# One term of a softmax denominator: slot 16 of three head groups summed by VectorE into the key sum instead of by TensorE with a column of ones

## The chip, the cores and the metric

One core of one Trainium2 chip. The metric is the device time of one execution in microseconds; less is better. Engines are called TensorE (PE in the rows; PEld is its weight load), VectorE (DVE), ScalarE (ACT), GpSimd (POOL) and SyncE (SP, here only a queue for transfers).

## What is computed

A post-norm transformer block on 2048 tokens of width 512 in float32. The part that matters here is the attention:

```python
qkv = (x @ w_qkv).reshape(B, S, 3, H, D)          # S = 2048, H = 16 heads, D = 32
q, k = _unit_norm(q), _unit_norm(k)               # and rotary embedding on the even heads
logits = jnp.einsum('bshd,bthd->bhst', q, k) * q_gain[None, :, None, None]
logits = jnp.where(causal[None, None], logits, jnp.finfo(logits.dtype).min)
attn = jax.nn.softmax(logits, axis=-1)
y = jnp.einsum('bhst,bthd->bshd', attn, v).reshape(B, S, Dm)
x = _layernorm(x + y @ w_out)
```

After it comes a mixture of experts (8 routed, top 2, and one shared) and a second layer norm. The change doesn't touch them.

## The kernel before

The 16 heads are worked on in four **groups** of four heads (g = 0 to 3). In a group, the 2048 queries are taken in four **steps** of 512 (i = 0 to 3), and the keys in blocks of 128 (j). A pair of a step and a key block is a **slot**. Causality leaves 4, 8, 12 and 16 key blocks for the four steps, so a group has 40 slots; `STEP_AT` gives the first slot of each step (0, 4, 12, 24) and `ORDER` the order of key blocks in a step. Slots 12 to 23 are the third step. Slot 16 is key block 4 of it, with all 512 queries and no mask.

For each slot:

- TensorE makes the **scores** of four heads, transposed: keys on partitions, 512 queries along the free axis (`pe_scores`, lines 1503 to 1534; the matmuls are line 1529). They go to two halves of PSUM, two heads each; the half p of a slot waits for the exponential of the same half of the slot before.
- ScalarE takes the **exponential** of each half into one of four buffers of `probs` (`act_exp`, lines 1669 to 1684). Before it overwrites a buffer it waits for the value matmuls and, by `sum_dve`, for the VectorE add of the slot four before.
- TensorE multiplies with v (`pe_values`, lines 1561 to 1582; line 1579), one slot behind the scores: its order is scores of slot n, projections and turns of this slot, values of slot n - 1.

The softmax also needs the **sum over the keys**, which lie on partitions and in many slots. A slot contributes in one of three ways:

- *Direct* (in `DIRECT`, or `DIRECT_LAST` for the last group): four matmuls with a block of ones (line 1576), ahead of the value matmuls, add its column sums into `sums_ps` in PSUM. A float32 matmul shows as two instructions, so there are eight.
- The first slot of a step that isn't direct is *first*: ScalarE writes its exponentials straight into `key_sum` instead of `probs`.
- Every later one that isn't direct is *added*: VectorE does `key_sum += probs` over four heads (`dve_add_keys`, lines 1800 to 1809; 128x2048 elements for a full slot).

At the end of a step TensorE adds `key_sum` into `sums_ps` with ones (`pe_sums`, line 1588), after waiting for the last VectorE add of the step, and ahead of the values of the last slot. In the third step slot 12 is direct, slot 13 is first, slots 14, 15 and 17 to 22 are added, and 16 and 23 are direct. The last group has another list, where 16 is added already.

Each engine runs a program of its own, slot by slot, written out in fixed tables:

- VectorE (lines 1860 to 1877): in a slot first the low half of a turned tile (`dve_turn_low`, line 1797; in groups 1 and 2 at slots 16 and 23, in group 0 at 16 and 24), then at the start of a step the reading and inverting of the sums (lines 1811 to 1829), the rotation, the add of the slot, the norms, and at slot 23 the high half of the split of the **next group's projection weights** (`dve_split_w`, line 1728).
- GpSimd: at slot 23 the causal mask on that slot's exponentials (`pool_mask`, line 1558), then the low half of the weight split (`pool_split_w`, line 1886), which waits for VectorE's high half. Masks of slots 20, 21 and 22 are made by TensorE (`MASK_BY_PRODUCT`, line 1532).
- TensorE: at slot 25 the first projection of the next group (`pe_project`, lines 1466 to 1484): three parts of four matmuls, the third of which waits for the low half of the weights.
- SyncE's queue: at slot 18 the load of those weights, and zero fills of a scratch tensor at slots 20 to 23.

The constants count too: `added(g, slot)` (line 1352) gives the value of `sum_dve` that each engine waits for, from the same lists.

Of the kernel before, what the change touches and what calls it, by code (L numbers as in the profile page):

```python
# [80 lines left out]

DIRECT = {0, 1, 2, 3, 4, 12, 16, 23, 24, 33, 37, 38, 39}
DIRECT_LAST = {0, 1, 2, 3, 5, 12, 13, 22, 24, 31, 32, 33, 38}
ADDING = [i for i in range(NC) if any(n not in DIRECT for n in range(STEP_AT[i], STEP_AT[i + 1]))]

# [14 lines left out]
def direct_of(g):  # L100

    return DIRECT_LAST if isinstance(g, int) and g == NG - 1 else DIRECT

# [50 lines left out]
def build(nc, x, x_across, w_qkv, w_out, q_gain, gate_w, w_gate, w_up, w_down, sw_gate, sw_up, sw_down,  # L154
          rope_cos, rope_sin, numbers, out):
    with ExitStack() as ctx:
# [1195 lines left out]
        def added(g, slot):  # L1352

            return (SLOTS - len(DIRECT) - len(ADDING)) * g + sum(n not in direct_of(g) and not is_first(g, n) for n in range(slot + 1))

        def is_first(g, slot):

            return slot not in direct_of(g) and slot == first_added(g, step_of(slot)[0])
# [598 lines left out]
```

How the kernel before makes its waits and increments, by code:

```python
        def load_piece(sp, lot, piece):  # L460
            if lot == 1:
                sp.wait_ge(lot0_low, piece + 1)
            if 1 < lot < LOTS - 1:
                sp.wait_ge(ffn_low, PIECES * (lot - 2) + piece + 1)
            if lot == LOTS - 1:
                sp.wait_ge(ffn_low, PIECES * (lot - 2) + (2, 3, 5)[piece])
            src, start = weights_of(lot)[piece], raw_at(lot, piece)
            to, n = raw[:, start:], src.shape[1]
            if piece < 2:
                sp.dma_start(to[:, 0:KC * n].rearrange("p (k n) -> p k n", k=KC), src.rearrange("(k p) n -> p k n", p=P)).then_inc(ffn_loaded[piece], 16)
            else:
                sp.dma_start(to[:, 0:2 * D].rearrange("p (k n) -> p k n", k=2), src[0:2 * P].rearrange("(k p) n -> p k n", p=P)).then_inc(ffn_loaded[piece], 16)
                for p0 in (0, MIXED) if lot == 0 else (0,):
                    sp.dma_start(to[p0:p0 + src.shape[0] - 2 * P, 2 * D:3 * D], src[2 * P:]).then_inc(ffn_loaded[piece], 16)
# [1 line left out]
        def tail_sync(sp):  # L477
            for n in range(2):
                sp.wait_ge(y_stored[n], 16 * NC * NG // 2)
            sp.wait_ge(y_ready, NC * NG)
            for t in range(TPC, 2 * TPC):
                load_x_row(sp, t)
            for t in range(2 * TPC, NT):
                if t >= TPC + 8:
                    sp.wait_ge(x1_ready, t - 7)
                load_x_row(sp, t)
                if t == 2 * TPC:
                    sp.wait_ge(sums_done, len(ADDING) * NG)
```

## Time and profile before

| | us |
|---|---|
| median of 3 runs | 1038.64 (1038.08 to 1041.03) |
| the profiled execution's own time | 1034.4 |
| its span, first to last instruction | 1032.7 |
| TensorE busy in the span | 999.6 (97%) |
| VectorE busy | 651.0 (63%) |
| ScalarE busy | 547.3 (53%) |
| GpSimd busy | 376.6 (36%) |

The profile is of one execution. "Busy" counts the time in which an engine has an instruction in work; matmuls are pipelined, so a busy TensorE is not one at its peak. "Idle before" is the time that an engine stood still ahead of an instruction, and the name behind it is what ended that. The chain of waits follows the work back from its last instruction to what released each step.

### The profile page before, as it was taken

How to read it: one execution, taken by the hardware profiler on the slowest of the kernel's cores; microseconds unless marked ns; L12 is line 12 of the kernel's file. 1: busy time of each engine (PE TensorE's matmuls, PEld its weight loads, DVE VectorE, ACT ScalarE, POOL GpSimd, SP SyncE). 2: the span in 40 equal slices, each digit the busy share in tenths (PEclk: the TensorE clock that was granted, in tenths of full speed). 3: DMA queues.
4: the chain of work that ended last, by engine and by line, in shares of the span. 5: the costliest groups of instructions: out<-in, count | busy, mean ns of one | idle time of the engine just before them, and what ended most of it. 6: DMA issues, size and time to landing. Idle time of an engine off the chain costs nothing.

```text
span 1032.7 us, 17543 instructions
## 1 busy us (share of the span) xinstructions
PE 999.6 (97%) x5951; PEld 724.4 (70%) x5951; DVE 651.0 (63%) x1138; ACT 547.3 (53%) x906; POOL 376.6 (36%) x312
## 2 busy tenths in 40 slices
PE   6899999999999999999999999999999999999996
PEld 7564566646666455664367778889999999998885
DVE  5699584896849968398679666444334333324776
ACT  4778776687767867668846632223333333321213
POOL 0332132321323312131534107563475666424431
PEclk9999999999999999999999999999999999999998
DMA  6447333473342723418146206593455553414433
GB/s 205 129 117 213 95 103 97 108 215 92 102 132 84 224 73 102 123 52 252 44 129 188 78 31 229 191 289 120 156 166 166 166 168 116 145 53 126 135 110 123
DMA packets 115821, 140.60 MB, mean 136 GB/s; under 512 B 10272, under 2 KB 74016, under 8 KB 115744
## 3 DMA queue, kind: packets, MB, share of 16 engines
q1 hardware_dynamic: 83552, 102.56, 33.4%
q10 hardware_dynamic: 27072, 20.20, 6.2%
q0 software_dynamic: 5120, 16.78, 5.0%
q8 instruction: 52, 0.85, 0.4%
q14 instruction: 25, 0.20, 0.1%
HBM read 83.93 MB, written 55.57 MB: 135 GB/s over the span
## 4 chain that ended last, share of the span: by engine, by line
PE 77%; DVE 10%; ACT 6%; DMA 2%; POOL 2%; issue 2%; SPq 0%; DVEq 0%; ACTq 0%
PE scores L634 15%; PE scores L1529 10%; PE bank L1482 10%; PE scores L694 8%; PE bank L1579 8%; PE bank L622 8%; PE bank L739 5%; PE scores L542 4%; ACT probs L1683 4%; DVE key_sum L1808 4%; PE bank L1576 3%; DVE x L1164 1%; PE scores L602 1%; POOL wqkv_l L1886 1%; PE bank L1588 1%
## 5 line engine op out<-in xcount | busy, mean ns | idle before, releaser
L1683 ACT ACTIVATE probs<-scores,shift_now 128x1024 f32<-128x1024 f32 (+3 forms) x296 | 273.5, 978 | 74.1 <-PE scores L1529 48.8
L1808 DVE TENSOR_TENSOR key_sum<-key_sum,probs 128x2048 f32<-128x2048 f32 (+1 forms) x96 | 205.3, 2138 | 50.7 <-PE bank L1579 19.1
L1529 PEld LDWEIGHTS scores<-q_stack,k_stack 96*128 96x128 f32 x624 | 99.2, 188 | 121.6 <-ACT probs L1683 66.1
L1529 PE MATMUL scores<-q_stack,k_stack 96*128 96x512 f32 (+3 forms) x624 | 177.1, 396 | 6.6 <-ACT probs L1683 2.8
L1579 PE MATMUL bank<-probs,v_sb 128*32 128x512 f32 (+3 forms) x1184 | 135.8, 533 | 0.0
L634 PE MATMUL scores<-ffn_w,xt_h 128*128 (+1 forms) x608 | 125.1, 328 | 0.0
L1044 DVE TENSOR_TENSOR ht_l<-scores,ht_h 128x256 fp32r<-128x256 f32 x39 | 16.6, 425 | 142.2 <-ACT ht_h L827 142.2
L634 PEld LDWEIGHTS scores<-ffn_w,xt_h 128*128 128x128 f32 x608 | 101.0, 189 | 3.5
L1263 POOL TENSOR_TENSOR ffn_w<-raw,ones 128x1408 fp32r<-128x1408 f32 (+4 forms) x32 | 64.1, 2014 | 97.6 <-PE bank L622 78.7
L1558 POOL TENSOR_SCALAR_AFFINE_SELECT probs<-probs 128x512 f32<-128x512 f32 x40 | 44.3, 1115 | 136.4 <-ACT probs L1683 136.4
L694 PE MATMUL scores<-x1T_h,ffn_w 128*128 128x512 f32 x352 | 89.5, 391 | 0.0
L1267 POOL TENSOR_TENSOR ffn_w<-raw,ffn_w 128x1408 fp32r<-128x1408 f32 (+3 forms) x31 | 80.3, 2600 | 1.9
L694 PEld LDWEIGHTS scores<-x1T_h,ffn_w 128*128 128x128 f32 x352 | 65.7, 188 | 13.5
L881 ACT CAST hid_h<-silu 128x512 fp32r<-128x512 f32 (+1 forms) x24 | 14.9, 620 | 105.7 <-DVE silu L1080 105.7
L622 PE MATMUL bank<-ffn_w,ht_h 128*128 (+2 forms) x234 | 67.6, 397 | 0.7 <-issue 0.7
L1579 PEld LDWEIGHTS bank<-probs,v_sb 128*32 128x32 f32 x1184 | 29.7, 109 | 47.0 <-issue 39.3
L634 PE MATMUL scores<-ffn_w,xt_l 128*128 (+1 forms) x304 | 61.0, 322 | 0.0
L834 ACT COPY y_tile<-bank 128x512 f32<-128x512 f32 x39 | 22.9, 587 | 69.3 <-PE bank L622 58.9
L1786 POOL TENSOR_TENSOR rope_prod<-qk_even,sin 128x128 f32<-128x128 f32 x8 | 4.5, 557 | 142.9 <-DVE qk_even L1775 142.9
L739 PE MATMUL bank<-ffn_w,hid_h 128*128 128x512 f32 x176 | 54.8, 394 | 1.4 <-DVE x L1132 1.1
L1327 POOL DMA_INDIRECT extra<-y_sorted,place_int x32 | 32.3, 1008 | 55.8 <-DMA y_sorted<-y_tile 20.9
L1482 PE MATMUL bank<-wqkv_h,xT_h 128*128 128x384 f32 x232 | 51.4, 343 | 0.9 <-DVE xT_l L1723 0.7
(254 smaller groups left out, 1760.2 us busy)
## 6 DMA issues: line engine op xcount, KB each, us to landing
k_stack<-turn_scratch SPq DMA_DIRECT2D x48, 256.0 KB, 4.3
q_stack<-turn_scratch SPq DMA_DIRECT2D x45, 256.0 KB, 3.9
x_sorted<-zeros SPq DMA_DIRECT2D x39, 256.0 KB, 3.5
y_sorted<-y_tile ACTq DMA_DIRECT2D x39, 256.0 KB, 2.9
x_tile<-x_sorted ACTq DMA_DIRECT2D x148, 64.0 KB, 2.0
turn_scratch<-turned_h SPq DMA_DIRECT2D x31, 256.0 KB, 2.1
turn_scratch<-turned_l SPq DMA_DIRECT2D x31, 256.0 KB, 2.3
raw<-w_gate SPq DMA_DIRECT2D x8, 704.0 KB, 5.2
```

Of the source, the lines that this page charges most:

```text
L622: mm = nc.tensor.matmul(out_tile[:], hs[0:kn, k, :], moving(slots[j - 1], DOWN + (low * 3 + k) * D, D, kn), start=(m == 0 and k == 0), sto ...
L634: mm = nc.tensor.matmul(to[:, 0:FH], xs[:, k, :], moving(slot, first + (low * KC + k) * FH, FH), start=(m == 0 and k == 0), stop=(m == 2 a ...
L694: mm = nc.tensor.matmul(scores[:, which, n % 2, :], stationary(half, slot, which, low, k, hc), xs[:, k, c * CH:(c + 1) * CH], start=(m == ...
L739: mm = nc.tensor.matmul(bank[n % 2][:], hs[:, k, tt * P:(tt + 1) * P], shared_down(half, slot, low, k), start=(k == 0 and hs is hid_h and ...
L1263: last = nc.gpsimd.tensor_tensor(high, src, one, ALU.mult)
L1267: last = nc.gpsimd.tensor_tensor(low, src, high.bitcast(F32), ALU.subtract)
L1482: mm = nc.tensor.matmul(qkv_bank(n)[:, 0:3 * P], xs[:, k, tok], ws[:, k, :], start=(m == 0 and k == 0), stop=(m == 2 and k == KC - 1))
L1529: mm = nc.tensor.matmul(scores[:, p, hh, lo:CH], k_stack[0:3 * HD, h, j * P:(j + 1) * P], q_stack[0:3 * HD, i % 2, h, lo:CH], start=True, ...
L1558: nc.gpsimd.affine_select(out=block, in_=block, compare_op=ALU.is_ge, fill=0.0, base=0, pattern=[[0, HG], [1, P]], channel_multiplier=-1). ...
L1579: mm = nc.tensor.matmul(y_ps[HD * h:HD * (h + 1), lo:CH], v_sb[:, j, HD * h:HD * (h + 1)], exponents(g, slot)[:, h, lo:CH], start=(slot == ...
L1683: nc.scalar.activation(exponents(g, slot)[:, 2 * p:2 * p + 2, lo:CH], scores[:, p, :, lo:CH], ACT.Exp, bias=shift_now[:, p:p + 1]).then_in ...
L1808: nc.vector.tensor_tensor(key_sum[:, :, lo:CH], key_sum[:, :, lo:CH], probs[:, slot % 4, :, lo:CH], ALU.add).then_inc(sum_dve, 1)
```

## The change

Slot 16 leaves the list of direct slots of the first three groups. By that alone its ones matmuls (line 1576) go from TensorE's program, and an add (line 1808) comes into VectorE's, between those of slots 15 and 17 and behind the turned tile of slot 16.

```diff
-DIRECT = {0, 1, 2, 3, 4, 12, 16, 23, 24, 33, 37, 38, 39}
+DIRECT = {0, 1, 2, 3, 4, 12, 23, 24, 33, 37, 38, 39}
 DIRECT_LAST = {0, 1, 2, 3, 5, 12, 13, 22, 24, 31, 32, 33, 38}
```

## Rows read from the trace of the kernel before

**Rows 1.** The page: busy time by engine, and the chain that ended last.

```profile
PE 999.6 (97%) x5951; PEld 724.4 (70%) x5951; DVE 651.0 (63%) x1138; ACT 547.3 (53%) x906; POOL 376.6 (36%) x312
...
PE 77%; DVE 10%; ACT 6%; DMA 2%; POOL 2%; issue 2%; SPq 0%; DVEq 0%; ACTq 0%
```

**Rows 2.** Windows, slots 12 to 23 of group 2: length, busy PE, PEld, DVE, ACT, POOL; clock, DMA.

```profile
327.00:357.00 30.00, 29.67 (x202) 12.49 (x202) 27.85 (x37) 25.40 (x31) 5.67 (x7) 1.00 0.60 173
```

**Rows 3.** Timeline, slots 14 to 22 of group 2: start, us, engine, line, operation.

```profile
337.98 5.01 DVE L1808 TENSOR_TENSOR key_sum<-key_sum,probs 128x2048 f32<-128x2048 f32 x2
...
341.75 1.06 PE L1576 MATMUL bank<-probs,ones 128*32 128x512 f32 x8
...
342.63 1.04 PE L1579 MATMUL bank<-probs,v_sb 128*32 128x512 f32 x8
...
343.60 1.21 PE L1529 MATMUL scores<-q_stack,k_stack 96*128 96x512 f32 x4
343.62 2.29 DVE L1808 TENSOR_TENSOR key_sum<-key_sum,probs 128x2048 f32<-128x2048 f32 x1
344.46 3.24 ACT L1683 ACTIVATE probs<-scores,shift_now 128x1024 f32<-128x1024 f32 x3 [0.87 <-PE scores L1529]
...
346.61 10.39 DVE L1808 TENSOR_TENSOR key_sum<-key_sum,probs 128x2048 f32<-128x2048 f32 x5 [0.69 <-ACT probs L1683]
```

**Rows 4.** The chain of waits, group 2, slots 19 to 25: start, us, what.

```profile
349.04 2.30 DVE key_sum L1808
...
357.61 0.88 DVE wqkv_h L1728
...
358.56 3.49 POOL wqkv_l L1886
```

**Rows 5.** Timeline, group 2, slots 23 to 27.

```profile
357.71 1.06 PE L1588 MATMUL bank<-key_sum,ones 128*32 128x512 f32 x8
...
362.09 0.97 PE L1482 MATMUL bank<-wqkv_l,xT_h 128*128 128x384 f32 x4 [0.33 <-POOL wqkv_l L1886]
...
369.28 2.29 DVE L1808 TENSOR_TENSOR key_sum<-key_sum,probs 128x2048 f32<-128x2048 f32 x1 [6.69 <-PE bank L1579]
```

**Rows 6.** Timelines of VectorE and TensorE, group 0, slots 18 to 25.

```profile
93.04 10.39 DVE L1808 TENSOR_TENSOR key_sum<-key_sum,probs 128x2048 f32<-128x2048 f32 x5 [0.68 <-ACT probs L1683]
103.35 1.39 DVE L1728 CAST wqkv_h<-wqkv_raw 128x1536 fp32r<-128x1536 f32 x1
...
108.38 0.96 PE L1482 MATMUL bank<-wqkv_l,xT_h 128*128 128x384 f32 x4 [0.24 <-POOL wqkv_l L1886]
```

**Rows 7.** Timeline of VectorE, group 1, slots 18 to 22.

```profile
220.13 2.29 DVE L1808 TENSOR_TENSOR key_sum<-key_sum,probs 128x2048 f32<-128x2048 f32 x1 [0.48 <-ACT probs L1683]
222.91 7.97 DVE L1808 TENSOR_TENSOR key_sum<-key_sum,probs 128x2048 f32<-128x2048 f32 x4 [0.48 <-DVE key_sum L1808]
```

**Rows 8.** GpSimd's mask, group 0; VectorE's cast by line; adds by form; adds in group 2.

```profile
102.78 1.15 POOL L1558 TENSOR_SCALAR_AFFINE_SELECT probs<-probs 128x512 f32<-128x512 f32 x1 [15.40 <-ACT probs L1683]
...
L1728 DVE CAST wqkv_h<-wqkv_raw x4: 950/956/1389, 6.7 to 357.5; 128x1536 fp32r<-128x1536 f32 x4
...
L1808 DVE TENSOR_TENSOR key_sum<-key_sum,probs 128x1536 f32<-128x1536 f32 x8 | 14.1, 1758 | 1.5 <-POOL probs L1558 0.5
...
319.18 7.01 DVE L1808 TENSOR_TENSOR key_sum<-key_sum,probs 128x2048 f32<-128x2048 f32 x3
```

**Rows 9.** TensorE's waits and its clock: timeline, then windows (columns as in rows 2).

```profile
428.22 1.19 PE L1529 MATMUL scores<-q_stack,k_stack 96*128 96x512 f32 x4 [2.16 <-DMA q_stack<-turn_scratch]
...
430.00:432.00 2.00, 2.00 (x21) 0.78 (x16) 0.00 (x0) 1.19 (x2) 0.00 (x0) 0.50 0.57 161
...
430.00:440.00 10.00, 10.00 (x71) 5.26 (x62) 5.10 (x13) 6.73 (x10) 0.00 (x0) 0.86 0.40 107
...
183.62 0.50 PE L1529 MATMUL scores<-q_stack,k_stack 96*128 96x256 f32 x2 [1.45 <-DMA k_stack<-turn_scratch]
...
183.00:189.00 6.00, 5.38 (x35) 4.15 (x36) 5.83 (x11) 3.48 (x5) 4.04 (x6) 1.00 0.23 66
```

## The prediction

> **What bounds the kernel now.** I read the page first. TensorE is busy for 97% of the span, and the chain that ended last is 77% TensorE but also 10% VectorE [rows 1]. So TensorE time is worth something on average, and the question is whether it is worth anything where slot 16 stands. The stretches come next: in the 30 us of slots 12 to 23 of the third head group TensorE is busy 29.67 us and VectorE 27.85 us at full clock [rows 2]. Two engines are close to full at the same time, so no share can decide; only the waits can.
>
> The timeline around slot 16 of the third group shows both sides [rows 3]. TensorE runs the ones matmuls of slot 16 from 341.75, the value matmuls from 342.63 and the scores of slot 18 from 343.60; ScalarE idles 0.87 us before the exponential of slot 18. That idle time is the ones matmuls' doing. VectorE finishes its two adds of slots 14 and 15 at 342.99 (337.98 + 5.01), does the low half of a turned tile, starts the add of slot 17 at 343.62, idles only 0.69 us and then runs five adds (slots 18 to 22) without a break for 10.39 us.
>
> The chain of waits says which side counts after that [rows 4]. After slot 18's exponential it is no longer on TensorE: it follows the key_sum adds to the last one, then the split of the next group's weights on VectorE, then the 3.49 us GpSimd half of that split. Then TensorE, which had waited for that weight [rows 5], carries on. The other two groups have the same row of adds, with other slack in front of it [rows 6, 7]. VectorE is therefore the bound from slot 18 to slot 25 in exactly the three groups that change.
>
> **The change, part by part.**
>
> Removed: in each of three groups the ones matmuls of slot 16, eight instructions that take 0.88 us of TensorE's order (341.75 to 342.63) [rows 3]; they overlap, so their spacing is the price and not the duration of one. Up to slot 23 TensorE and ScalarE gain it: the exponential of slot 18 loses its 0.87 us wait. Slot 12 stays the first direct slot of its step and slot 13 the first one in key_sum, so no start flag and no owner of key_sum moves. No DMA is added, removed or moved in any queue. The last group has a list of its own, in which 16 was already absent, and doesn't change.
>
> Added: one 128x2048 add in each of three groups. The add of slot 17 takes 2.29 [rows 3]. Of the five that run back to back the first starts at 346.61 and the second at 349.04 [rows 3, 4], 2.43 later, so a gap of some 0.13 belongs to each. The new add costs 2.42 in all. Its operand is long ready (the ones matmuls of slot 16, which read the same exponentials, started at 341.75), so it stands right before the add of slot 17, with no wait of its own.
>
> Behind it on VectorE are queued the adds of slots 17 to 22, the turned tile, the weight split, and the reading of the sums. What absorbs the 2.42 is the idle time before those adds, less the usual 0.13 each. Third group: 0.69 - 0.13 = 0.56 before slot 18, none later; the last add ends 1.86 later. First group: 0.68 - 0.13 = 0.55 [rows 6], 1.87 later. Second group: 0.48 - 0.13 = 0.35 before slot 18, and the same again before slot 19 [rows 7]. That second idle follows an add directly and nothing explains it; if it vanishes in a full queue the shift is 1.72, if it stays 2.07. I take 1.72.
>
> Buffers: the exponential of slot n needs the add of slot n - 4. With ScalarE 0.87 earlier and VectorE 1.86 later, slot 24 would start at about 356.6 and needs the add of slot 20, which ends at about 355.6. The margin is 1 us, so that wait costs nothing; if ScalarE didn't gain, it would be larger still.
>
> First consumer, **the sum over key_sum** (line 1588). In the third group it starts at 357.71 [rows 5]. TensorE would now arrive at 356.8, but the add of slot 22 ends at 357.00 + 1.86 = 358.86 (357.00 is 346.61 + 10.39). So it starts about 1.2 later than before, and TensorE idles 2 us: the 0.88 gained is gone here.
>
> Second consumer, **the weight split**. VectorE's cast and then GpSimd's subtraction follow the last add in order, so GpSimd ends at 358.56 + 3.49 + 1.86 = 363.9 [rows 4]. TensorE's third part of the projection started at 362.09, after waiting [rows 5]; without the wait of 0.33 and with the late sum it would be due at 361.8 + 1.2 = 363.0, so it waits for GpSimd again, 0.9 us, and starts 1.86 late. Everything behind it (values of slot 24, scores of slot 26, the projections of slots 26 to 28) is in TensorE's order, and VectorE idles 6.69 us there waiting for TensorE [rows 5], so nothing gives the time back. In the first group TensorE waited only 0.24 us for the same weight at 108.38 [rows 6], but it did wait, so the shift passes in full.
>
> One more term: **the mask of slot 23 on GpSimd.** Now it falls beside the last add (102.78, 1.15 us), and in the first group the cast after it takes 1.39 where the median of the cast is 0.96 [rows 6, 8]. With exponentials 0.87 earlier it falls beside the add of slot 20 and gets in before that of slot 21. The nearest row is three adds in 7.01 us [rows 8]; two full ones, one of three quarters (1.76) and two gaps would be 2.29 + 1.76 + 2.29 + 0.26 = 6.60, so 0.41 is the price of a mask that gets in. Bounds 0 and 0.41 for each group; in the first group an add's 0.41 only takes the place of the cast's 0.43, so 0. I take 0.41 in the other two, since adds stand without a break there. The Trainium skill ("SBUF — State Buffer", section "SBUF: two separate sides") says that a VectorE instruction with two SBUF inputs and a GpSimd instruction that reads SBUF shut each other out for a whole instruction, whichever starts first; by it a mask that starts ahead of an add would hold that add for the mask's full unhindered length and not for a part. The row agrees in kind (adds beside masks took longer) and doesn't tell the length.
>
> Sum: 1.87 + 1.72 + 0.41 + 1.86 + 0.41 = 6.27 us slower. The profiled execution took 1034.4 us (span 1032.7), so the changed one should show 1040.7 (span 1039.0). The median of the three runs is 1038.64, 4.2 above the profiled execution; the same 6.3 on top gives 1044.9.
>
> **The rivals.**
>
> *A: VectorE is hidden and the TensorE time is gained.* Then 3 x 0.88 = 2.6 faster, 1036.0. For it: TensorE is busy 97%, and ScalarE's 0.87 wait is real. Against: the chain leaves TensorE at 346.6 and comes back only at 362.1 [rows 4]. It would hold if more than 1.86 us of slack lay between the last add and the projection; the trace shows a wait there instead. This is the case on the other side; its point of decision is whether TensorE still waits for the GpSimd half of the weights. Chance 0.06.
>
> *B: only the sum's wait counts.* If the weight split had slack, each group would lose 1.2: 3.6 in all, 1042.2. For it: the wait for the weight was small (0.24 in the first group). Against: small is not absent. Chance 0.1.
>
> *C: the losses cancel or the later stretch absorbs them*, as when a DMA or the next step's adds set the pace: near 1038.6. Against: slots 25 to 28 wait for TensorE alone. Chance 0.1.
>
> *D: TensorE's clock falls.* In the last group TensorE idled 2.16 us for a q_stack transfer, and from 430 to 432 the granted clock was 0.50, its lower level of 1.2 GHz; over 430 to 440 it was 0.86 [rows 9]. The change makes a new idle of about 2 us in front of the sum (2.5 with the mask) and one of 0.9 before the projection. The price: 10 x (1 - 0.86) = 1.4 us of full clock, say 1.5, of which 0.9 is hidden by the wait for the weight; if it fell later, 1.5 each. That is 6.3 + 3 x 0.6 to 6.3 + 3 x 1.5, or 1046.7 to 1049.4. Against: a wait of 1.45 us in the second group, at 183.62, was followed by a clock of 1.00 [rows 9]. Chance 0.14. The Trainium skill ("TensorE: Matmul & The Clock Gate", Part 1) has idle time return the clock to the lower level; the last group agrees, and the rule speaks against this change.
>
> *E: the change does nothing*: the constant is read by every engine's program, so this can't be. My own forecast keeps 0.6.
>
> **How the numbers follow.** A measurement of this kernel can tell about 0.3%, 3.1 us, from no change. Slower by more: the forecast, D and most of B: 0.8. Within: C, part of B and a low forecast: 0.14. Faster by more takes A with some luck: 0.06. The range: the low end takes B and the lower bounds (5.45, no mask) with the runs' own scatter of 1 to 2 us, 1040.5; the high end takes D to 1048.5. A, C and the worst of D are left out, some 0.2.
>
> **What would show it.** Right: ScalarE's idle before slot 18 gone; VectorE with seven adds in an unbroken row from slot 16; TensorE waiting about 2 us for key_sum before line 1588 in three groups, and longer than before (some 1 us) for the GpSimd weight at line 1482; slots 0 to 15 of each group unchanged in length; the last group unchanged. Wrong: the third projection part starting as long after the scores of slot 15 as before; a granted clock below 1 in slots 23 to 27 would be D.

## The result, and the profile after

The changed kernel takes 1042.07 us (median of 20 runs, 1039.92 to 1049.14) against 1037.78 (20 runs, 1034.00 to 1041.03): ratio 1.0043, 95% interval 1.0029 to 1.0056. That is 4.3 us slower. A second set on another chip (below) gave 1039.78 against 1033.76, ratio 1.0066 (1.0050 to 1.0082), 6.0 us; one more execution of the changed kernel there took 1383.26 us at a mean granted clock of 0.66 and is left out of these figures. (The ratios are not quotients of the medians and can differ a little from them.) Slower was forecast, by 6.3; the 1044.9 of the forecast stood on the 1038.64 of three runs, where 20 runs give 1037.78.

The page of the profiled execution after, to set beside [rows 1]:

```profile
span 1042.7 us, 17501 instructions
...
PE 1000.3 (96%) x5927; PEld 725.8 (70%) x5927; DVE 658.6 (63%) x1141; ACT 547.8 (53%) x906; POOL 376.1 (36%) x312
...
PE 70%; DVE 15%; ACT 5%; DMA 4%; issue 2%; POOL 1%; SPq 0%; DVEq 0%; ACTq 0%; another core or an unknown queue 0%
```

TensorE has 24 matmul instructions less and VectorE three adds more; VectorE's share of the chain that ended last went from 10 to 15%, and DMA's from 2 to 4%. The span grew by 10.0, far more than the median time. Half of that isn't the change's. From the last exponential to the end (the mixture of experts) it took 507.1 us before and 512.0 after, but 506.6 in the second profile of the changed kernel; over the 13 profiles of this case it lies anywhere from 506.1 to 512.1, and why is open. I therefore compare the attention part alone: from the first exponential to that of the last slot it grew by 6.0 us in both profiles of the changed kernel.

The timeline of the third group after, VectorE first, then TensorE and ScalarE (start us, duration us, what, and the idle time before with what ended it):

```profile
344.19 5.01 DVE L1808 TENSOR_TENSOR key_sum<-key_sum,probs 128x2048 f32<-128x2048 f32 x2
...
349.72 15.65 DVE L1808 TENSOR_TENSOR key_sum<-key_sum,probs 128x2048 f32<-128x2048 f32 x7
...
365.89 0.95 DVE L1728 CAST wqkv_h<-wqkv_raw 128x1536 fp32r<-128x1536 f32 x1
...
347.70 4.24 ACT L1683 ACTIVATE probs<-scores,shift_now 128x1024 f32<-128x1024 f32 x4
...
365.43 1.35 PE L1588 MATMUL bank<-key_sum,ones 128*32 128x512 f32 x8 [2.22 <-DVE key_sum L1808]
366.54 0.68 PE L1576 MATMUL bank<-probs,ones 128*32 128x128 f32 x8
...
367.57 2.06 PE L1529 MATMUL scores<-q_stack,k_stack 96*128 96x512 f32 x4
...
370.89 0.86 PE L1482 MATMUL bank<-wqkv_l,xT_h 128*128 128x384 f32 x4
```

ScalarE runs slots 17 and 18 (four halves) without the 0.87 us wait of [rows 3]: TensorE's time was gained there, as forecast. VectorE now has seven adds in one unbroken row from slot 16, and TensorE stands still for 2.22 us at line 1588 until the last of them is done. So far this is the prediction. But then the matmuls are slow (0.68 us for a group that took 0.40 before, scores 2.06 instead of 1.20), and the third part of the projection doesn't wait for GpSimd at all.

The second group shows why, in the windows (length, busy PE, PEld, DVE, ACT, POOL, granted clock, DMA):

```profile
232.00:234.00 2.00, 0.00 (x0) 0.00 (x0) 1.87 (x2) 1.26 (x2) 0.00 (x0) 0.74 0.05 17
234.00:236.00 2.00, 1.81 (x12) 0.50 (x16) 1.61 (x3) 0.00 (x0) 0.31 (x1) 0.50 0.22 79
236.00:238.00 2.00, 2.00 (x23) 1.40 (x16) 0.92 (x2) 0.58 (x1) 2.00 (x1) 0.50 0.59 185
238.00:240.00 2.00, 2.00 (x8) 1.81 (x7) 1.62 (x3) 1.75 (x2) 1.14 (x1) 0.56 0.02 7
```

and in the timeline of TensorE and GpSimd there:

```profile
234.19 1.94 PE L1588 MATMUL bank<-key_sum,ones 128*32 128x512 f32 x8 [2.71 <-DVE key_sum L1808]
...
235.69 3.45 POOL L1886 TENSOR_TENSOR wqkv_l<-wqkv_raw,wqkv_h 128x1536 fp32r<-128x1536 f32 x1 [4.52 <-DVE wqkv_h L1728]
...
240.65 0.86 PE L1482 MATMUL bank<-wqkv_l,xT_h 128*128 128x384 f32 x4
```

After 2.71 us of waiting TensorE works for over 5 us at a granted clock of 0.50, the lower of its two levels (1.2 GHz). GpSimd is ready at 239.14 and TensorE comes to the weight only at 240.65. The slow clock has taken the place of the wait for the weight. In the first group of this profile the clock stayed at 1.00 behind a wait of 2.27 us.

**A measure for the stretch in question.** From the exponentials in each trace I took the time from the start of slot 17's to the start of slot 26's, and the difference to the same in the trace before, for groups 0, 1 and 2 (before: 24.07, 24.59 and 24.23 us):

| kernel | group 0 | group 1 | group 2 | sum |
|---|---|---|---|---|
| forecast | 1.87 | 2.13 | 2.27 | 6.27 |
| changed, first profile | 1.74 | 3.59 | 2.45 | 7.78 |
| changed, second profile | 2.57 | 2.51 | 2.44 | 7.52 |
| changed, TensorE kept busy in the wait, first | 1.70 | 1.90 | 2.15 | 5.75 |
| the same, second | 1.79 | 1.90 | 2.16 | 5.85 |
| add only | 1.63 | 1.95 | 1.94 | 5.52 |
| changed, low half of the weights by VectorE | 1.02 | 1.97 | 2.15 | 5.15 |
| neither matmul nor add | -0.57 | -0.11 | -0.56 | -1.24 |
| slot 21 in place of 16 | 0.04 | 0.53 | -0.07 | 0.50 |
| before, low half of the weights by VectorE | -0.47 | -0.94 | -0.58 | -1.99 |
| changed, TensorE's program padded at slot 16 | 2.69 | 2.54 | 1.92 | 7.14 |
| before, 24 small matmuls in the opening | 0.01 | -0.02 | 0.00 | -0.01 |
| before, both mendings | -0.51 | -0.97 | -0.61 | -2.08 |

### The profile page after: what moved, and what is told of

Its sections match the earlier page's. It is cut to its first block, busy times and chain, and to the rows that moved or that the text cites. A ratio compares the mean times of both kernels' runs of the same rounds, so it can differ in the third digit from the quotient of the medians.

```text
span 1042.7 us, 17501 instructions
## 1 busy us (share of the span) xinstructions
PE 1000.3 (96%) x5927; PEld 725.8 (70%) x5927; DVE 658.6 (63%) x1141; ACT 547.8 (53%) x906; POOL 376.1 (36%) x312
## 4 chain that ended last, share of the span: by engine, by line
PE 70%; DVE 15%; ACT 5%; DMA 4%; issue 2%; POOL 1%; SPq 0%; DVEq 0%; ACTq 0%; another core or an unknown queue 0%
PE scores L634 14%; PE scores L1529 9%; PE bank L1482 8%; PE bank L622 8%; PE scores L694 8%; PE bank L1579 7%; DVE key_sum L1808 6%; PE bank L739 5%; PE scores L542 4%; ACT probs L1683 4%; PE bank L1576 2%; DMA q_stack<-turn_scratch 2%; DVE x L1164 1%; DMA turn_scratch<-turned_l 1%; PE scores L602 1%
## 5 line engine op out<-in xcount | busy, mean ns | idle before, releaser
L1808 DVE TENSOR_TENSOR key_sum<-key_sum,probs 128x2048 f32<-128x2048 f32 (+3 forms) x99 | 213.1, 2152 | 51.3 <-PE bank L1579 20.9
```

Of the source, the lines that this page charges most:

```text
L1808: nc.vector.tensor_tensor(key_sum[:, :, lo:CH], key_sum[:, :, lo:CH], probs[:, slot % 4, :, lo:CH], ALU.add).then_inc(sum_dve, 1)
```

## The experiments

The theory: VectorE's queue from slot 16 to the weight split is late by the add, and through the key sum and the weights so is TensorE. Rivals: TensorE's work is the bound (A), only the sum's wait counts (B), the clock (D). Each experiment's ratio is to the kernel before on the same chip.

### The two halves of the change, one at a time

Neither the ones matmuls nor the add, so slot 16 is missing from the sum of three groups (against the kernel before):

```diff
-            if slot in direct_of(g):
+            if slot in direct_of(g) and slot != 16:
                 first = ...
```

> Slot 16 of the first three groups is left out of the softmax sum altogether: no ones matmuls, no add. VectorE theory (the chain from slot 18 to the weight split is VectorE's): TensorE's 0.88 us is gained only as far as the adds can start earlier, about 0.56 us per group (the idle time before slot 18's add less its usual gap), so 1 to 2.6 us faster than before in all. Rival A (TensorE is the bound throughout): 2.6 us faster. If it is no faster at all, something else, such as the clock, is at work.

Measured: 1033.31 against 1037.80, ratio 0.9954 (0.9940 to 0.9969), 4.5 us faster. The stretch gained only 1.24 us in three groups, not 2.6, and VectorE's row of six adds (slots 17 to 22) starts right behind the turned tile and fills the queue from there:

```profile
343.45 0.68 DVE L1797 TENSOR_TENSOR turned_l<-bank,turned_h 128x512 fp32r<-128x512 f32 x1
344.16 12.82 DVE L1808 TENSOR_TENSOR key_sum<-key_sum,probs 128x2048 f32<-128x2048 f32 x6
```

Even with the work gone altogether, only 0.57, 0.11 and 0.56 us of TensorE's 0.88 per group come through. That settles A in the stretch. The 4.5 us in all were more than any theory had; the rest of them lies elsewhere, in the last group (below).

Both the matmuls and the add, so slot 16 is counted twice in three groups (against the changed kernel):

```diff
-            if slot in direct_of(g):
+            if slot in direct_of(g) or (slot == 16 and g < NG - 1):
                 first = ...
```

> Both the ones matmuls and the add for slot 16 (it is counted twice in the sum of the first three groups). VectorE theory: nearly as slow as the changed kernel, 4 to 7 us above before, since the 0.88 us of TensorE that the change saves lies behind the same VectorE queue; the idle time of TensorE before line 1588 is only 1.2 us instead of 2.2 to 2.7, so the granted clock should stay at 1.00 in slots 23 to 26 and the later loss with it. Rival (TensorE's work and VectorE's work both count fully): 2.6 us slower than the changed kernel.

Measured: 1043.73 against 1037.80, ratio 1.0058 (1.0037 to 1.0079), 5.9 us slower; stretch 5.52. The clock stayed up behind the shorter wait, and both waits of the forecast stand there in a clean form:

```profile
363.11 1.07 PE L1588 MATMUL bank<-key_sum,ones 128*32 128x512 f32 x8 [1.21 <-DVE key_sum L1808]
...
368.13 0.96 PE L1482 MATMUL bank<-wqkv_l,xT_h 128*128 128x384 f32 x4 [1.00 <-POOL wqkv_l L1886]
```

The add alone costs nearly what the change costs where the clock stays up (5.52 beside 5.75 and 5.85 in the table); what the change takes from TensorE is worth nothing there.

### The clock

Twelve matmuls whose result is thrown away, ahead of the wait for the key sum in three groups:

```diff
         def pe_sums(g, i):
-
+            pe_fill(g, i)
             nc.tensor.wait_ge(sum_dve, added(g, STEP_AT[i + 1] - 1))
...
+        def pe_fill(g, i):
+            if i == 2 and g < NG - 1:
+                nc.tensor.wait_ge(qkv_copied, NT * (g + 1))
+                for _ in range(12):
+                    nc.tensor.matmul(qkv_ps[:, 0:3 * P], xT_h[:, 0, 0:P], xT_h[:, 1, 0:3 * P], start=True, stop=True)
```

> The changed kernel with twelve idle matmuls (their result is thrown away) in TensorE's order ahead of the wait for the key sum, about 2.1 us, so TensorE works through the wait. If the clock (rival D) is part of the loss: granted clock 1.00 in slots 23 to 26 of all three groups and 1 to 4 us faster than the changed kernel, so 2 to 5 us above before. If only the VectorE chain counts: the same time as the changed kernel, 4 to 6 us above before.

Measured: 1045.15 against 1037.80, ratio 1.0067 (1.0045 to 1.0089). In the stretch it did what rival D said. The second group of that profile, timeline of TensorE:

```profile
231.02 2.27 PE L1596 MATMUL bank<-xT_h 128*128 128x384 f32 x12
233.53 1.07 PE L1588 MATMUL bank<-key_sum,ones 128*32 128x512 f32 x8 [0.23 <-DVE key_sum L1814]
...
238.55 0.97 PE L1482 MATMUL bank<-wqkv_l,xT_h 128*128 128x384 f32 x4 [0.98 <-POOL wqkv_l L1892]
```

TensorE works through the wait, the ones matmuls take 1.07 and not 1.94, and it reaches the weight early enough to wait 0.98 us for it. The stretch costs 5.75 instead of 7.78. Yet the whole kernel wasn't faster than the changed one's 1.0043. So it was run again beside the changed kernel on one chip.

> The changed kernel unaltered, a second profile and more runs of it beside the others of this set. If the fall of the clock at the wait for the key sum is the rule, groups 1 and 2 show 0.50 again; if it is a matter of chance, another pattern. Time: 4 to 6 us above before.

Measured, the changed kernel unaltered: 1039.78 against 1033.76, ratio 1.0066 (1.0050 to 1.0082). The idle times before line 1588 were 2.25, 2.71 and 2.22 us and the clock fell behind all three (0.75, 0.68 and 0.61 in windows of two microseconds of work behind them). Which of them are hit varies. Over the attention parts of all 13 profiles, TensorE had 18 waits of 1.81 to 2.71 us; the clock fell at 13 of them (1.93 to 2.71) and stayed at 1.00 at five (1.81, 1.84, 1.91, 2.24 and 2.27). It fell at none of the shorter ones, the longest 1.59.

> The changed kernel with twelve idle matmuls in front of the wait, again, now beside the changed kernel on the same chip. Its three steps of slots 17 to 26 took 1.70, 1.90 and 2.15 us more than before's, those of the changed kernel 1.74, 3.59 and 2.45, so if runs of the changed kernel usually see the clock fall it is 0 to 2 us faster than the changed kernel here; if the fall is rare, the same within 1.5 us.

Measured: 1039.78 against 1033.76, ratio 1.0064 (1.0049 to 1.0080): the same as the changed kernel in time, though its stretch is 1.7 us shorter (5.85 against 7.52). Part of the answer is that the changed kernel gets time back elsewhere, which is the subject of the fetches, below; six runs of each can't tell a difference of 1 to 2 us. The profiles don't agree on the whole: the attention part is longer than before's by 6.0 us in the first filled profile, where the clock fell in the last group, and by 3.3 in the second, where it didn't, beside 6.0 of the changed kernel in both. So the clock's price is shown in the stretch; that the whole kernel pays it is not.

### The load on VectorE, not the slot

Slot 21, of 384 queries, direct in place of slot 16 (against before):

```diff
-DIRECT = {0, 1, 2, 3, 4, 12, 16, 23, 24, 33, 37, 38, 39}
+DIRECT = {0, 1, 2, 3, 4, 12, 21, 23, 24, 33, 37, 38, 39}
```

> Slot 21 (384 queries) is direct in place of slot 16, so VectorE gets a 2.42 us add and loses a 1.89 us one, and TensorE gives up 0.88 us and takes some 0.65. VectorE theory: the last add ends when it did before within 0.1 us (1.86 - 1.89), TensorE hardly waits, the loss is gone: within 1 us of before. Rival (the change is slow because of slot 16 leaving TensorE, or for the count of adds before slot 17): still 3 us or more slower.

Measured: 1037.64 against 1037.80, ratio 1.0001 (0.9985 to 1.0016). The same engines' programs with slot 16 added as in the change, but one add less behind it: no loss. VectorE's row ends in time and TensorE doesn't wait at line 1588:

```profile
342.42 13.33 DVE L1808 TENSOR_TENSOR key_sum<-key_sum,probs 128x2048 f32<-128x2048 f32 x6
...
356.28 1.06 PE L1588 MATMUL bank<-key_sum,ones 128*32 128x512 f32 x8
```

The loss is the length of VectorE's queue ahead of the sum.

### The second consumer: the weight split

VectorE does the low half too, right behind the high one, in place of GpSimd:

```diff
-        def dve_first_w_low():
-            nc.vector.wait_ge(w_high, 1)
+        def dve_first_w_low(g=0):
+            nc.vector.wait_ge(w_high, g + 1)
...
                     if slot == SPLIT_W_AT and has_following(g):
                         dve_split_w(g + 1)
+                        dve_first_w_low(g + 1)
...
-                    if slot == SPLIT_W_AT and has_following(g):
-                        pool_split_w(g + 1)
```

In the changed kernel:

> The changed kernel, with the low half of the weight split done by VectorE right after the high half (about 1.7 us) in place of GpSimd's 3.49 us, in three groups. Forecast's theory (the late weight sets the loss, 1.86 per group): it is ready 1.8 us earlier, so only the wait for the key sum is left, 1.2 (1.6 with the mask) per group: 3 to 5 us above before, 1 to 3 us faster than the changed kernel. Rival B (only the sum's wait counts in the changed kernel): no faster than the changed kernel.

Measured: 1038.46 against 1033.76, ratio 1.0053 (1.0039 to 1.0066), beside 1.0066 of the changed kernel in the same set: 1.3 us less by the medians, though the intervals overlap. The stretch costs 5.15 instead of 7.52, 1.02 of it in the first group (where 1.2 was forecast for the sum alone) and some 2 in the others, where the clock fell again behind waits of 2.35 and 2.22 us. The first group is the clean comparison, since the clock stayed up there in this profile and in the first of the changed kernel: 1.02 against 1.74. So the weight's part is real, and B as a sole cause is not the case; but the slow clock hides most of the gain in the other two.

In the kernel before:

> The kernel before with the same edit to the weight split. The waits of TensorE for the late weight (0.24, 0.67, 0.33 us) go: about 1 us faster than before if the theory holds, and a candidate that beats both; if VectorE's reading of the sums becomes late instead, no gain or a loss of up to 1 us per group.

Measured: 1031.76 against 1033.76, ratio 0.9984 (0.9971 to 0.9996), 2.0 us faster, stretch -1.99. VectorE's low half takes 1.76 us where GpSimd's took 3.49, and TensorE's third part starts without a wait, 0.72 behind the second:

```profile
357.20 1.76 DVE L1732 TENSOR_TENSOR wqkv_l<-wqkv_raw,wqkv_h 128x1536 fp32r<-128x1536 f32 x1
...
359.60 0.88 PE L1482 MATMUL bank<-wqkv_h,xT_l 128*128 128x384 f32 x4
360.32 0.86 PE L1482 MATMUL bank<-wqkv_l,xT_h 128*128 128x384 f32 x4
```

Some 1 us had been expected from the idle times before the third part (0.24, 0.67 and 0.33). They understate how late it was, for they count from the end of the second part, and the parts start 0.70 to 0.72 us apart where nothing waits. Before, in the third group, they start 1.20 apart (362.09 in [rows 5] less 360.89):

```profile
360.89 0.87 PE L1482 MATMUL bank<-wqkv_h,xT_l 128*128 128x384 f32 x4
```

By that measure the third part was late by 0.39, 0.84 and 0.50 us, 1.7 in all. The chain in [rows 4] was the bound before the change already, as the prediction read it.

### What gave time back: a late store, and fetches of instructions

By slots, the kernels differ in one more place: slots 3 to 5 of the last group. Before, TensorE waits 2.16 us for q_stack at slot 4 and the clock falls [rows 9]; in both profiles of the changed kernel, in the one without matmul and add, and in the changed one with VectorE's low half, this is gone, and from the first exponential of slot 3 to that of slot 5 it takes 6.7 to 6.8 us there instead of 10.4. Instead they wait 1.2 to 1.6 us at slot 4 of the third group. The kernel before, slot 21, add only, before with VectorE's low half and the filled ones wait in the last group (8.5 us from slot 3 to slot 5 where the clock stays up, 10.2 to 10.4 where it falls). The first lot has 48 instructions of TensorE (matmuls and weight loads) less than before, the second as many or more.

The chain of waits of the kernel before, then of the changed one, both in the last group:

```profile
418.73 4.04 DMA turn_scratch<-turned_l
```

```profile
427.41 2.01 DMA turn_scratch<-turned_l
```

The same 256 KB store landed after 4.04 us and after 2.01. In the DMA queues of that stretch the first has a packet of another kind beside it (queue: packets, MB, share of time), and the second has none:

```profile
q1 hardware_dynamic: 288, 0.52, 34.7%
q8 instruction: 1, 0.02, 2.8%
...
turn_scratch<-turned_l SPq DMA_DIRECT2D x1, 256.0 KB, 4.0
```

Queue 8's packets are 16 KB of instructions each; there are 52 in the whole profile before and 51 in the one after. By the trace's record of packets, the one at 418.9 us took 1.83 us, at the start of that store (418.73); in the third group of the changed kernel one at 296.9 took 1.60 and the store from 297.19 landed after 3.42:

```profile
297.19 3.42 DMA turn_scratch<-turned_l
```

To test whether they are TensorE's fetches and do the harm, two kernels move them.

The changed kernel with eight small matmuls at slot 16, so that TensorE's program is as long as before's:

```diff
+            if slot == 16 and g < NG - 1:
+                nc.tensor.wait_ge(qkv_copied, NT * (g + 1))
+                for _ in range(8):
+                    nc.tensor.matmul(qkv_ps[:, 0:P], ident_b[:], mask_b[:], start=True, stop=True)
             if slot in direct_of(g):
```

> The changed kernel with eight small bf16 matmuls (result thrown away, about 0.5 us) in the place of the eight ones matmuls of slot 16, so TensorE's program is as long as before's. Theory of the fetches (a 16 KB packet of TensorE's instructions that falls beside the store of a turned tile makes that store land 1.4 to 2.2 us late): the fetches go back to before's slots, so the late store returns in the last group (TensorE waits some 2 us for q_stack at slot 4) and goes from the third: 1 to 3.5 us slower than the changed kernel, 7 to 9 us above before. Rival (chance): the pattern of the changed kernel, third group late and last group not, and its time.

Measured: 1041.37 against 1033.79, ratio 1.0070 (1.0049 to 1.0090). The pattern went over as expected: no wait at slot 4 of the third group, and in the last group the store landed late and TensorE waited 1.91 us. The chain of waits there:

```profile
425.67 4.00 DMA turn_scratch<-turned_l
...
430.58 4.29 DMA q_stack<-turn_scratch
```

The time doesn't tell it from the changed kernel's 1.0066, measured on another chip, so the 1 to 3.5 us above the changed kernel that were expected aren't shown; the pattern is.

The kernel before with 24 small matmuls in TensorE's opening:

```diff
             pe.wait_ge(consts_ready, 1)
+            nc.tensor.wait_ge(triangle_made, 1)
+            for _ in range(24):
+                nc.tensor.matmul(y_ps[:, 0:P], ident_b[:], mask_b[:], start=True, stop=True)
             for kind, n in OPENING:
```

> The kernel before with 24 small bf16 matmuls (thrown away) in TensorE's idle opening, which moves each of its instruction fetches 48 instructions forward, about 4 us. Theory of the fetches: the store of the last group's turned q tile lands in 2.0 us and not in 4.0, the wait of 2.16 us for q_stack and the fall of the clock behind it go, 2 to 4 us faster than before, unless another store is hit. Rival: no difference.

Measured: 1029.97 against 1033.79, ratio 0.9959 (0.9945 to 0.9973), 3.8 us faster by adding 24 useless matmuls. The packet of the last group moved from 418.9 to 414.3 us, of which the schedule's own shift is 1.1; in its DMA view the store lands in 2.0 again, and in its timeline TensorE passes from the turn to slot 4's scores without a wait:

```profile
turn_scratch<-turned_l SPq DMA_DIRECT2D x1, 256.0 KB, 2.0
```

```profile
424.36 0.60 PE L1499 MATMUL bank<-ident,qk_odd 128*128 128x128 f32 x4
424.96 1.19 PE L1529 MATMUL scores<-q_stack,k_stack 96*128 96x512 f32 x4
```

From slot 3 to slot 5 of the last group it took 3.8 us less than before, and slots 3 to 7 of the second 1.53 less.

The 13 profiles can be compared at one and the same store. The last group's store from 418.73 before has an instruction packet of queue 8 that starts between 0.1 us ahead of it and 0.4 behind it in seven of them (before, add only, both filled ones, slot 21, before with VectorE's low half, the padded one), and lands in 3.91 to 4.04 us; in the other six there is none beside it, and it lands in 2.00 to 2.01. The third group's equal store (297.19 after) has one in four (both of the changed kernel, the one without matmul and add, the changed one with VectorE's low half) and lands in 3.42 to 3.66, and without one in nine, in 2.00 to 2.02. This doesn't make a packet the only cause of a late landing, nor a sure one: other stores of this size land after 2.7 to 5.4 us with no packet beside them, and the store just ahead of the last group's, with the same packet beside it, lands in 2.55 to 2.57 and not in 2.01 to 2.04.

### Both mendings together

The kernel before with VectorE's low half and the 24 small matmuls.

> The kernel before with VectorE doing the low half of the weight split and the 24 small matmuls in the opening. If both act by themselves: 2 us (split) and 2 to 4 us (fetches), 4 to 6 us faster than before, and the version that beats both kernels. If the shift of the schedule by the split moves the stores onto other fetches, only the 2 us of the split.

Measured: 1027.83 against 1033.79, ratio 0.9939 (0.9921 to 0.9956), 6.0 us faster: the stretch gained 2.08, and slot 3 to slot 5 of the last group 4.0. This version beats both kernels.

## Why the prediction was right, and where not

**TensorE's 0.88 us, gained up to slot 23 and lost at line 1588**: right. ScalarE's wait before slot 18 went, and TensorE waited 2.2 to 2.7 us for the key sum, where 2 to 2.5 was forecast; the kernel with neither matmul nor add gained 1.24 us in three stretches, not 2.6.

**The add, 2.42 less what idle time absorbs**: right in kind. VectorE's seven adds took 15.44, 15.79 (with an idle 0.48) and 15.65 us. The unexplained idle in the second group, which I let vanish, came back, one add earlier (0.48 before slot 17).

**The mask**: mis-sized. Seven adds and six gaps would be 5 x 2.29 + 1.76 + 1.22 + 6 x 0.13 = 15.21, so the mask took 15.44 - 15.21 = 0.23 in the first group, 0.23 in the second (its idle 0.48 counted as a usual gap) and 0.44 in the third; I had 0, 0.41 and 0.41, so the three together are nearly right (0.90 against 0.82). In the first group the cast took 0.95 instead of 1.39, as forecast. That the row of adds with a mask beside it is longer than its parts is shown; the Trainium skill's rule ("SBUF — State Buffer", "SBUF: two separate sides") of a lock for a whole instruction is in line with that, and the rows don't tell how much of the mask's length the add had to wait.

**Two consumers, sum and weight**: right. Without the clock in play (filled, and add only) the stretches cost 1.6 to 1.8, 1.9 and 1.9 to 2.2 where I had 1.87, 2.13 and 2.27, 0.4 to 0.8 us too much in all; and the wait for the weight was 0.97 to 1.00 in the second and third groups where I had 0.9, and 0.4 in the first. My reading that the third part was due at 361.8 took the idle time for the lateness; by the spacing of the parts it was due at 361.6. The sum doesn't rest on it.

**The clock, rival D**: the term that failed, and the one that had been put at nothing in the sum. I kept it apart from the forecast with a chance of 0.14, since an earlier wait of 1.45 us had left the clock up. The waits of 2.2 to 2.7 us brought it down in two groups of three in one profile and in all three in the other, at 7.5 to 7.8 us for the three stretches against 5.8 of the filled kernel: a term of 1.7 to 2.0 us that belonged in the sum. Its price was right: 0.6 for a group where the wait for the weight hides the rest, which over three groups is 1.8. The Trainium skill's statement that idle time returns the clock to the lower level ("TensorE: Matmul & The Clock Gate", Part 1) bore on this change after all, and the traces agree: 0.50 behind five of these six waits.

**"The last group unchanged"**: wrong, and so are "slots 0 to 15 unchanged" and "nothing gives the time back". TensorE's program was 48 instructions shorter by the last group, an instruction packet no longer fell beside that group's store, and the 2.16 us wait and the fall of the clock went with it, 3.7 us; the third group gained a wait of 1.2 to 1.6, and slots 3 to 5 of the first took 0.5 to 1.0 longer. In the first profile that is 7.78 - 3.71 + 1.31 + 0.46 and 0.17 of small differences, 6.0 us for the attention part. The errors nearly cancel (6.27 was forecast), and that is luck: the size came out well for reasons that were only in part mine. The first set's 4.3 us lies below that; the runs don't tell whether the chip or the rest of the kernel makes the difference between 4.3 and 6.0.

**A, B, C**: A fell with the removal kernel and with add only. B fell with the kernels whose low half went to VectorE (2.0 us faster before the change by an edit that leaves the key sum alone, and 1.02 against 1.74 in the first group after it). C, that something gives time back, was true in part and in a form that I hadn't thought of: 3.7 us in the last group, and not enough to bring the time near 1038.6.

## What to carry to other kernels

Before work moves from a busy engine to another, follow the receiving engine's queue from the new instruction to the next point where the first one waits for it; if that queue has less idle time than the instruction is long, the saving comes back as a wait, and a wait of some 2 us can bring a slow clock with it (it did at 13 of the 18 waits of 1.8 to 2.7 us in these profiles). When small edits to TensorE's program give gains or losses in stretches that they don't touch, compare the landing times of equal transfers, and look for an instruction packet beside the late one. A loss of this kind may be mended at the consumer: giving the weight split's low half to VectorE gained 2.0 us in the kernel before (in the changed one the 1.3 us lie within the noise).

## What was not expected of the hardware

- Two 256 KB stores from SBUF to DRAM that landed in 2.0 us in 15 cases landed in 3.4 to 4.0 in the 11 in which a 16 KB instruction packet fell beside the start. Adding 24 small matmuls far ahead moved that packet away and made the whole kernel 3.8 us faster (0.9959, 0.9945 to 0.9973). That the two share one of the 16 DMA engines is my reading of it, and not shown; the traces show the coincidence and its end, not the engine.
- TensorE at 0.50 needed 1.94 us for the ones matmuls over key_sum that take 1.06 otherwise, and where the clock was low it no longer waited for a weight that was itself late.
- VectorE subtracts 128x1536 in 1.76 us where GpSimd takes 3.49, so the kernel was 2.0 us faster (0.9984, 0.9971 to 0.9996) with that half on the engine that the chain showed as the bound.
